# A graph network on one Trainium2 core: the first group's weights, messages and low parts put in another order

## The chip, the core and the metric

The kernel runs on one core of one Trainium2 chip. The metric is the device time of one execution in microseconds (us), the median of several runs. The engines are named as the profile names them: PE (TensorE: matrix products, PEld its weight loads), DVE (VectorE), ACT (ScalarE), POOL (GpSimd), SP (SyncE, which here only issues transfers). Each engine runs its own instructions in the order of the program and waits on semaphores for the others.

## What is computed

The inputs are 32 graphs of 256 nodes with 128 features (`x`) and a 256 by 256 adjacency matrix for each (`adj`), all in 32-bit floating point. The reference, cut to what matters:

```python
x = layernorm(x + gnn0(x, adj));  x = layernorm(x + gnn1(x, adj))

# gnn0
h = relu(bn1(conv1d(xc, conv1_w, pad=0)))          # xc: x with features first
h = bn2(conv1d(h, conv2_w, pad=8))                 # 17 taps along the 256 nodes
x_conv = relu(h + xc)
s = x @ w_se.T + b_se                              # 3 numbers a node
A = exp(-squared_distance(s, s)) * adj
x_nmp = A @ relu(x @ w_msg.T + b_msg)              # messages
gi = concat(x_conv, x_nmp) @ w_ih.T + b_ih;  gh = x @ w_hh.T + b_hh
r, z = sigmoid(gi_r + gh_r), sigmoid(gi_z + gh_z)
out0 = (1 - z) * tanh(gi_n + r * gh_n) + z * x

# gnn1
out1 = relu(((1 + eps) * x + adj @ x) @ W1 + b1) @ W2 + b2
```

## The kernel before

**Groups and steps.** The 32 graphs are handled in 8 groups of 4. The work on a group has a front (first convolution, 17-tap convolution, messages, distances, message sum) and a back (gates, the two norms, the adjacency product, the two-layer net). A prologue does the front of group 0 alone and begins that of group 1; step s then does the back of group s-1 between pieces of the front of group s; a last part does the back of group 7. In each engine's program the order is written out by hand in the functions `prologue`, `steady` and `last`; nothing but semaphores ties the engines together.

**High and low parts.** A large product is done as three products of rounded operands: every 32-bit operand is split into a high part (made by ACT, functions with `high` in their name, tiles `wh`, `xh`, `sth`, `w1h`) and the rest, the low part (a subtraction, so far always on DVE: `wl`, `xl`, `stl`, `w1l`). PE takes high x high, low x high and high x low, in `products` (line 1074).

**The 17 taps.** The convolution is cut into nine smaller ones, `taps(g, n)` for n from 0 to 8, of 4 or 5 taps each, three on each of three streams of data (M, A, B). Their weights are the taps themselves (`c2raw`, in the space of `tail`), sums of two neighbours (`msum`, in the space of `gbuf`) and sums in the tile `qsum` (in the space of `adjT[1]`): slots 0 to 4, 5 to 9 and 10 to 13. The prologue makes these sums, then for each n the high part (`tap_high(n)`, ACT) and the low part (`tap_low(n)`, DVE); PE waits for the n-th low part on the semaphore `w_low`. The streams are the relu of the first convolution (`h1_out` on ACT, tile `h1`) and differences of it that POOL makes: `split_diff` (tile `dx`, two instructions), `diff_a` and `diff_b` (tile `dv`). Their parts are made by `odd_high`, `diff_high`, `odd_low` and `diff_low`.

**What else POOL does.** It multiplies the exponentials with the adjacency matrix (`mask`, four a group) and adds 1 + eps to the diagonal of the adjacency matrix (`add_diagonal`, four a group, 128x256).

**The end of the prologue.** PE does the first convolution of group 1 (`conv1(1, 1, 0)` and `conv1(1, 1, 1)`) and the message sums (`nmp`), between the last taps of group 0. ACT writes the two halves of group 1's `h1` from it (line 578). Before the first taps of group 1 PE waits for the low parts of the gate weights (`graw`, nine slots, 128x1152) and of W1 (128x256), the 11th and 12th count of `w_low`; both are subtractions on DVE.

**Transfers.** SP issues all loads and stores, ACT only the load of the identity matrix. The order on SP is: vectors and first weights, x of group 0 in two halves, the 17 taps (`c2raw`, 1088 KB), later weights, adjacency of group 0, gate weights, x of group 1.

## Time and profile before

| | us |
|---|---|
| median of three runs (lowest, highest) | 415.11 (414.59, 415.78) |
| the profiled execution's own time | 415.75 |
| span of its trace | 413.9 |
| PE busy | 380.0 (92%) |
| DVE busy | 309.7 (75%) |
| POOL busy | 224.3 (54%) |
| ACT busy | 211.1 (51%) |

The span is what the trace covers, from the first instruction to the last; the execution's own time is longer by what lies around it, 1.85 us here. Busy times are of the span. PE shows busy during most of it, but a row of PE lasts until its modelled end while the next has begun, so the spacing of its rows tells more than their length.

### The profile page before, as it was taken

Reading aid. Unit: us, or ns where it says so; the run is one execution under the profiler, and the core shown is the slowest. Engines: PE = TensorE matmul, PEld = TensorE weight load, DVE = VectorE, ACT = ScalarE, POOL = GpSimd, SP = SyncE. Lnnn points to the kernel's source line nnn. Section 1 sums busy time; section 2 is a strip of 40 time slices with the busy share of each in tenths; the row PEclk is TensorE's granted clock in tenths of the full one; section 3 lists DMA queues with packets and bytes.
Section 4 is the critical chain, followed back from the end, with each engine's and each line's share of the span. In section 5 each row is a group of like instructions: output and inputs, shape, how many; then the busy total and the mean of one; then the engine's idle time right before and its main releaser. Section 6 shows DMA issues by size and latency. Waiting matters only on the chain.

```text
span 413.9 us, 6658 instructions
## 1 busy us (share of the span) xinstructions
PE 380.0 (92%) x2369; PEld 338.3 (82%) x2369; DVE 309.7 (75%) x599; ACT 211.1 (51%) x366; POOL 224.3 (54%) x215
## 2 busy tenths in 40 slices
PE   2479999998999999998999999999999999999974
PEld 1478888898898898988898988988988988989864
DVE  3878847879588885888688795878768795867665
ACT  3637456642755337443566427653484436461641
POOL 2536544848357464657349473565556573495252
PEclk9989999999999999999999999999999999999999
DMA  7302001110012000130012010120001300000101
GB/s 270 155 2 102 2 1 51 41 64 25 26 52 103 24 29 0 53 101 25 25 51 73 29 44 7 51 101 25 27 6 46 104 25 28 1 2 0 52 0 51
DMA packets 7561, 19.40 MB, mean 47 GB/s; under 512 B 625, under 2 KB 4977, under 8 KB 6385
## 3 DMA queue, kind: packets, MB, share of 16 engines
q1 hardware_dynamic: 7392, 19.02, 13.2%
q8 instruction: 14, 0.23, 0.2%
q14 instruction: 11, 0.08, 0.1%
q10 hardware_dynamic: 144, 0.07, 0.1%
HBM read 14.89 MB, written 4.19 MB: 46 GB/s over the span
## 4 chain that ended last, share of the span: by engine, by line
PE 57%; DVE 23%; issue 8%; POOL 5%; ACT 4%; DMA 2%; SPq 0%; DVEq 0%; POOLq 0%; ACTq 0%
PE back L1074 28%; PE conv L1074 14%; PE back L1236 6%; DVE tail L882 5%; POOL rstd L472 4%; PE front L1149 3%; DVE xn L882 3%; PE front L1121 2%; DMA tail<-in_conv_dram 2%; DVE esum L839 2%; DVE usum L843 2%; DVE usum L827 2%; DVE wl L925 1%; DVE stats L872 1%; DVE stl L765 1%
## 5 line engine op out<-in xcount | busy, mean ns | idle before, releaser
L1074 PE MATMUL conv<-sth,wh 128*128 128x256 f32 x320 | 99.5, 311 | 16.5 <-DVE stl L765 13.1
L1074 PE MATMUL conv<-stl,wh 128*128 128x256 f32 x320 | 92.8, 290 | 0.0
L1074 PE MATMUL conv<-sth,wl 128*128 128x256 f32 x320 | 92.7, 290 | 0.0
L1074 PEld LDWEIGHTS conv<-sth,wh 128*128 128x128 f32 x320 | 62.2, 194 | 20.6 <-DVE wl L925 10.4
L472 POOL TENSOR_TENSOR rstd<-rstd,minus_half 128x4 f32<-128x4 f32 (+1 forms) x34 | 36.1, 1062 | 65.2 <-DVE rstd L876 65.2
L1074 PEld LDWEIGHTS conv<-stl,wh 128*128 128x128 f32 x320 | 62.3, 195 | 1.0
L1074 PEld LDWEIGHTS conv<-sth,wl 128*128 128x128 f32 x320 | 62.1, 194 | 0.0
L477 POOL TENSOR_TENSOR xw<-xw,xv 128x512 f32<-128x512 f32 (+1 forms) x17 | 20.9, 1228 | 62.0 <-ACT xw L640 62.0
L490 POOL TENSOR_TENSOR amat<-amat,adjT 128x512 f32<-128x512 f32 x32 | 48.1, 1525 | 5.1 <-ACT amat L616 4.2
L882 DVE TENSOR_SCALAR tail<-tail,stats,rstd 128x128 f32<-128x128 f32 x64 | 41.4, 709 | 0.0
L647 ACT ACTIVATE xch<-usum 128x512 fp32r<-128x512 f32 x16 | 10.1, 631 | 40.7 <-DVE usum L843 40.7
L455 POOL TENSOR_TENSOR dx<-dv 128x272 f32<-128x272 f32 x16 | 14.7, 916 | 29.8 <-DVE stl L765 29.8
L1149 PE MATMUL front<-amat,msg 128*128 128x256 f32 x128 | 30.2, 379 | 0.0
L1236 PE MATMUL back<-later_w,tail 128*128 128x128 f32 x240 | 29.2, 275 | 0.0
L1149 PE MATMUL back<-adjT,xn 128*128 128x256 f32 x120 | 29.1, 385 | 0.0
L1236 PEld LDWEIGHTS back<-later_w,tail 128*128 128x128 f32 x240 | 28.6, 192 | 0.6
L578 ACT ACTIVATE h<-conv,bn 128x512 f32<-128x512 f32 x16 | 12.5, 781 | 27.6 <-PE conv L1074 27.1
L1149 PEld LDWEIGHTS front<-amat,msg 128*128 128x128 f32 x128 | 23.7, 189 | 3.2
L622 ACT ACTIVATE msg<-msg 128x384 f32<-128x384 f32 (+1 forms) x24 | 10.9, 484 | 29.8 <-DVE msg L785 29.4
L848 DVE SCALAR_TENSOR_TENSOR xcl<-usum,xch 128x512 fp32r<-128x512 f32 x16 | 22.2, 1388 | 4.9 <-ACT xch L647 4.9
L858 DVE TENSOR_TENSOR gbuf<-back,gbuf 128x512 f32<-128x512 f32 x14 | 9.7, 692 | 20.6 <-PE back L1074 20.6
L765 DVE TENSOR_TENSOR stl<-dx,sth 128x544 fp32r<-128x544 f32 x24 | 17.7, 737 | 9.8 <-ACT sth L565 9.7
(198 smaller groups left out, 987.1 us busy)
## 6 DMA issues: line engine op xcount, KB each, us to landing
adjT<-in_adj_dram SPq DMA_DIRECT2D x8, 1024.0 KB, 4.8
out_dram<-tail SPq DMA_DIRECT2D x15, 256.0 KB, 2.2
xv<-in_x_dram SPq DMA_DIRECT2D x7, 512.0 KB, 3.3
tail<-in_conv_dram SPq DMA_DIRECT2D x1, 1088.0 KB, 8.2
gbuf<-in_gates_dram SPq DMA_DIRECT2D x1, 576.0 KB, 11.8
xv<-in_x_dram SPq DMA_DIRECT2D x2, 256.0 KB, 3.0
later_w<-in_later_dram SPq DMA_DIRECT2D x1, 452.0 KB, 8.9
out_dram<-tail SPq DMA_DIRECT2D x2, 128.0 KB, 1.9
```

Of the source, the lines that this page charges most:

```text
L455: done(pool.tensor_tensor(dx[:, 0, :, :], ev, od, ALU.subtract), DX_READY[st])
L472: done(pool.tensor_tensor(rstd[:, k, h, q], rstd[:, k, h, q], minus_half[:, q], ALU.pow), RSTD[k])
L477: done(pool.tensor_tensor(xw[:, h, part(c)], xw[:, h, part(c)], xv[u][:, part_cols(h, c)], ALU.mult), XWX_READY)
L490: done(pool.tensor_tensor(amat[:, b, :, :], amat[:, b, :, :], adjT[u][:, b, :, :], ALU.mult), A_READY)
L578: done(act.activation(h1[:, 2 * h:2 * h + 2, :, :, PAD:PAD + TQ].rearrange("p b r q m -> p (b r) q m"), conv1_bank(h)[:, :].rearrange("p ( ...
L622: done(act.activation(msg_blocks[:, q0:q1, :], msg_blocks[:, q0:q1, :], ACT.Relu), MSG_READY)
L765: done(dve.tensor_tensor(dst, src, full(hi), ALU.subtract), name)
L848: done(dve.scalar_tensor_tensor(xcl[:, :, par, :], pre[:, :, par, :], 0.0, full(xch[:, :, par, :]), ALU.max, ALU.subtract), XCL_READY)
L882: last = dve.tensor_scalar(dst(q), src(q, q + 1), stats[:, k, h, q, 1:2], rstd[:, k, h, q:q + 1], ALU.subtract, ALU.mult)
L1074: ins = pe.matmul(bank, a, b, start=first and k == 0, stop=last and k == len(todo) - 1)
L1149: ins = pe.matmul(tile[:, k * N:(k + 1) * N], lhs(b, rm), rhs(b, rm), start=rm == 0, stop=rm == PAR - 1)
L1236: ins = pe.matmul(bank("out", h, c)[:, k * P:(k + 1) * P], hid[:, h, f, q * P:(q + 1) * P], w2[:, f, :], start=f == 0, stop=f == 1)
```

## The change

**Transfers.** The 17 taps come in four transfers, two issued by SP and two by ACT ahead of the identity matrix, all counted on `conv2_loaded`. SP waits for all four before it issues the adjacency matrix, x of group 1 and (now after x) the gate weights.

**Messages.** PE does group 0's messages right after the first convolution, ahead of the first taps, and the transposed factors ahead of `taps(0, 3)`. DVE's additions on the messages stand between the first low parts.

**Sums and low parts.** The two sums of 512 elements for `qsum` slots 5 to 8 and 10 to 13 go from DVE to POOL, as do the low parts of the gate weights and of W1. Those two have a semaphore of their own, `w_gate_low`, and PE waits for its second count where it waited for the 12th of `w_low`.

**Order.** On POOL two masks of group 0 stand ahead of the last `split_diff` of group 0. On ACT and DVE several parts move, among them both halves of group 1's x (`x_high`, `x_low`) ahead of the last difference of group 0's stream B, and the constant `diag` to a later place.

The core of the diff:

```diff
@@ SP
-                sp.dma_start(c2raw, t["conv2"]).then_inc(conv2_loaded, 16)
+                sp.dma_start(c2raw[:, 0:5, :], t["conv2"][:, 0:5, :]).then_inc(conv2_loaded, 16)
+                sp.dma_start(c2raw[:, 5:9, :], t["conv2"][:, 5:9, :]).then_inc(conv2_loaded, 16)
                 sp.dma_start(later_w[:, :], t["later"]).then_inc(later_loaded, 16)
+                sp.wait_ge(conv2_loaded, 64)
                 load_adj(0, 0)
-                sp.dma_start(graw, t["gates"]).then_inc(gates_loaded, 16)
                 wait(sp, X_LOADED, 0, 16)
                 load_x(1, 1)
+                sp.dma_start(graw, t["gates"]).then_inc(gates_loaded, 16)
@@ POOL
                 split_diff(0, 0)
+                pool.wait_ge(conv2_loaded, 64)
+                pool.tensor_tensor(qsum[:, 5:9, :], c2raw[:, 0:TAPS - 1:4, :], c2raw[:, 2:TAPS:4, :],
+                                   ALU.add).then_inc(tap_sums_ab, 1)
                 diff_a(0)
+                pool.tensor_tensor(qsum[:, 10:14, :], c2raw[:, 1:TAPS:4, :], c2raw[:, 3:TAPS:4, :],
+                                   ALU.add).then_inc(tap_sums_ab, 1)
                 split_diff(0, 1)
                 diff_b(0)
+                mask(0, 0, 0)
+                mask(0, 0, 1)
                 split_diff(0, 2)
-                for b in range(GB):
-                    mask(0, 0, b)
-                pool.wait_ge(bn_ready, 3)
+                mask(0, 0, 2)
+                mask(0, 0, 3)
+                pool.wait_ge(w_high, 11)
+                pool.tensor_tensor(wl[:, S_GATE:S_GATE + 9, :], graw, full(wh[:, S_GATE:S_GATE + 9, :]),
+                                   ALU.subtract).then_inc(w_gate_low, 1)
                 split_diff(1, 0)
                 diff_a(1)
                 split_diff(1, 1)
                 diff_b(1)
+                pool.wait_ge(bn_ready, 3)
                 for b in range(GB):
                     add_diagonal(0, 0, b)
+                pool.wait_ge(w_high, 12)
+                pool.tensor_tensor(w1l[:, :], w1raw, full(w1h[:, :]), ALU.subtract).then_inc(w_gate_low, 1)
@@ ACT
+                act.dma_start(c2raw[:, 9:13, :], t["conv2"][:, 9:13, :]).then_inc(conv2_loaded, 16)
+                act.dma_start(c2raw[:, 13:TAPS, :], t["conv2"][:, 13:TAPS, :]).then_inc(conv2_loaded, 16)
                 act.dma_start(ident, t["consts"]).then_inc(consts_loaded, 16)
@@ DVE
-                dve.wait_ge(gates_loaded, 16)
-                w_low_part(wl[:, S_GATE:S_GATE + 9, :], graw, wh[:, S_GATE:S_GATE + 9, :], 11)
-                w_low_part(w1l[:, :], w1raw, w1h[:, :], 12)
@@ PE
                 conv1(0, 0, 1)
+                pe.wait_ge(later_loaded, 16)
+                messages(0, 0)
                 pe.wait_ge(w_low, 2)
                 taps(0, 0)
                 pe.wait_ge(w_low, 3)
                 taps(0, 1)
-                pe.wait_ge(later_loaded, 16)
-                messages(0, 0)
                 pe.wait_ge(w_low, 4)
                 taps(0, 2)
+                pe.wait_ge(consts_loaded, 16)
+                factors(0)
                 pe.wait_ge(w_low, 5)
                 taps(0, 3)
-                pe.wait_ge(consts_loaded, 16)
-                factors(0)
...
                 nmp(0, 1)
                 taps(0, 8, 1)
-                pe.wait_ge(w_low, 12)
+                pe.wait_ge(w_gate_low, 2)
```

POOL, from the last differences of group 0 to the first instruction of step 1 (tile `xw`), before. `amat` are the masks of group 0, `dx` and `dv` the differences (ahead of the masks those of group 0, behind them those of group 1), `diag` is 1 + eps on the diagonal; in brackets stand the semaphores that an instruction waits for.

```order
L455 TENSOR_TENSOR dx<-dv 128x272 [waits streamA_ready,h1_diff_ready]
L456 TENSOR_TENSOR dx<-dv 128x272
L490 TENSOR_TENSOR amat<-amat,adjT 128x512 [waits adj_loaded,exp_ready] x4
L455 TENSOR_TENSOR dx<-h 128x272 [waits streamB_ready,h1_ready,bn_ready]
L456 TENSOR_TENSOR dx<-h 128x272
L461 TENSOR_TENSOR dv<-h 128x544 [waits streamA_ready,h1_ready]
L455 TENSOR_TENSOR dx<-dv 128x272 [waits streamM_ready,h1_diff_ready]
L456 TENSOR_TENSOR dx<-dv 128x272
L465 TENSOR_TENSOR dv<-h 128x4x68 [waits streamB_ready]
L466 TENSOR_TENSOR dv<-h 128x4x68
L498 TENSOR_TENSOR adjT<-adjT,diag 128x2x128 [waits a_ready] x4
L477 TENSOR_TENSOR xw<-xw,xv 128x512 [waits x_weight_ready]
```

The same place after the change, from behind the last two masks on, with line numbers of the changed file.

```order
L530 TENSOR_TENSOR wl<-gbuf,wh 128x1152 [waits w_high]
L459 TENSOR_TENSOR dx<-h 128x272 [waits streamB_ready,h1_ready]
L460 TENSOR_TENSOR dx<-h 128x272
L465 TENSOR_TENSOR dv<-h 128x544 [waits streamA_ready,h1_ready]
L459 TENSOR_TENSOR dx<-dv 128x272 [waits streamM_ready,h1_diff_ready]
L460 TENSOR_TENSOR dx<-dv 128x272
L469 TENSOR_TENSOR dv<-h 128x4x68 [waits streamB_ready]
L470 TENSOR_TENSOR dv<-h 128x4x68
L502 TENSOR_TENSOR adjT<-adjT,diag 128x2x128 [waits a_ready,bn_ready]
L502 TENSOR_TENSOR adjT<-adjT,diag 128x2x128 [waits a_ready] x3
L540 TENSOR_TENSOR w1l<-later_w,w1h 128x256 [waits w_high]
L481 TENSOR_TENSOR xw<-xw,xv 128x512 [waits x_weight_ready]
```

What moved: the gate weights' low part (`wl`) stands between the masks and group 1's first differences, and W1's low part (`w1l`) is the last instruction of POOL's prologue, behind group 1's differences and the four diagonal additions. The masks, four in a row in the first list, stand two ahead of and two behind the first list's first two rows.

DVE, from the sums of the taps to the first difference's low part, before. `adjT` holds the tile `qsum` here, `gbuf` the tile `msum`, `tail` the taps.

```order
L954 TENSOR_TENSOR gbuf<-tail 128x1024 [waits conv2_loaded]
L956 COPY gbuf<-tail 128x128
L957 COPY adjT<-tail 128x2x128
L959 TENSOR_TENSOR adjT<-gbuf 128x512 [waits tap_pairs]
L960 TENSOR_TENSOR adjT<-tail 128x512
L961 TENSOR_TENSOR adjT<-tail 128x512
L925 TENSOR_TENSOR wl<-adjT,wh 128x640 [waits w_high]
L765 TENSOR_TENSOR stl<-h,sth 128x272 [waits streamM_high_ready]
L925 TENSOR_TENSOR wl<-gbuf,wh 128x640 [waits w_high]
L925 TENSOR_TENSOR wl<-gbuf,wh 128x512 [waits w_high]
L765 TENSOR_TENSOR stl<-dx,sth 128x544 [waits streamM_high_ready]
```

After, from the third sum on (`msg` and `fact` are the additions on the messages):

```order
L976 TENSOR_TENSOR adjT<-gbuf 128x512 [waits tap_pairs]
L806 TENSOR_TENSOR msg<-front,later_w 128x384 [waits msg_full,factors_set,later_loaded]
L808 TENSOR_TENSOR fact<-front,later_w 128x6x3
L946 TENSOR_TENSOR wl<-adjT,wh 128x640 [waits w_high]
L786 TENSOR_TENSOR stl<-h,sth 128x272 [waits streamM_high_ready]
L806 TENSOR_TENSOR msg<-front,later_w 128x384 [waits msg_full]
L808 TENSOR_TENSOR fact<-front,later_w 128x6x3
L946 TENSOR_TENSOR wl<-gbuf,wh 128x640 [waits w_high]
L806 TENSOR_TENSOR msg<-conv,later_w 128x256 [waits msg_full]
L808 TENSOR_TENSOR fact<-conv,later_w 128x4x3
L946 TENSOR_TENSOR wl<-gbuf,wh 128x512 [waits w_high]
L786 TENSOR_TENSOR stl<-dx,sth 128x544 [waits streamM_high_ready]
```

What moved: two sums have left DVE, and the additions on the messages, which stood behind the last row of the first list, stand between the low parts.

## Rows read from the trace of the kernel before

**Rows 1.** Windows, one step: stretch, length, busy by engine, granted clock, DMA, GB/s.

```profile
143.41:191.52 48.11, 46.74 (x293) 41.59 (x293) 37.44 (x71) 25.16 (x43) 27.50 (x25) 1.00 0.14 45
```

**Rows 2.** PE's timeline: start, length, line, tiles, count, [idle before, releaser].

```profile
15.52 0.55 PE L1074 MATMUL conv<-sth,wh 128*128 128x256 f32 x1 [6.74 <-DVE stl L765]
...
28.11 0.55 PE L1074 MATMUL conv<-sth,wh 128*128 128x256 f32 x1 [2.78 <-DVE wl L925]
...
36.24 0.39 PE L1074 MATMUL conv<-sth,wh 128*128 128x256 f32 x1
...
40.41 0.47 PE L1074 MATMUL conv<-xh,wh 128*128 128x512 f32 x1 [0.97 <-DVE xl L765]
```

**Rows 3.** PE's timeline, first taps of group 1 (first, last) and the next.

```profile
46.78 0.28 PE L1074 MATMUL conv<-sth,wh 128*128 128x256 f32 x1
...
48.48 0.28 PE L1074 MATMUL conv<-sth,wl 128*128 128x256 f32 x1
49.46 0.36 PE L1074 MATMUL conv<-sth,wh 128*128 128x256 f32 x1 [0.69 <-DVE esum L839]
```

**Rows 4.** Windows, columns as in rows 1: PE at its slower pace.

```profile
15.50:21.30 5.80, 5.57 (x25) 5.32 (x26) 3.62 (x3) 3.94 (x8) 4.47 (x5) 1.00 0.01 5
...
28.15:31.55 3.40, 3.40 (x17) 3.40 (x18) 3.40 (x5) 0.00 (x0) 1.93 (x2) 0.55 0.02 5
```

**Rows 5.** ACT's timeline: first exponentials of group 0; second half of group 1's h1.

```profile
34.24 1.09 ACT L616 ACTIVATE amat<-front 128x512 f32<-128x512 f32 x2 [0.42 <-PE front L1141]
...
44.15 0.78 ACT L578 ACTIVATE h<-conv,bn 128x512 f32<-128x512 f32 x1 [0.44 <-PE conv L1074]
```

**Rows 6.** POOL's timeline: masks of group 0, then group 1's differences and the diagonals.

```profile
34.92 6.49 POOL L490 TENSOR_TENSOR amat<-amat,adjT 128x512 f32<-128x512 f32 x4 [4.20 <-ACT amat L616]
...
45.06 0.76 POOL L455 TENSOR_TENSOR dx<-h 128x272 f32<-128x272 f32 x1 [3.65 <-issue]
...
48.79 0.76 POOL L455 TENSOR_TENSOR dx<-dv 128x272 f32<-128x272 f32 x1 [0.73 <-DVE stl L765]
...
52.60 2.79 POOL L498 TENSOR_TENSOR adjT<-adjT,diag 128x256 f32<-128x256 f32 x4
```

**Rows 7.** DVE's timeline in the first group.

```profile
10.40 1.22 DVE L954 TENSOR_TENSOR gbuf<-tail 128x1024 f32<-128x1024 f32 x1 [3.27 <-DMA tail<-in_conv_dram]
...
13.08 0.68 DVE L961 TENSOR_TENSOR adjT<-tail 128x512 f32<-128x512 f32 x1
13.68 0.82 DVE L925 TENSOR_TENSOR wl<-adjT,wh 128x640 fp32r<-128x640 f32 x1
...
22.89 0.56 DVE L785 TENSOR_TENSOR msg<-front,later_w 128x384 f32<-128x384 f32 x1 [3.77 <-PE front L1121]
...
33.85 0.73 DVE L765 TENSOR_TENSOR stl<-dx,sth 128x544 fp32r<-128x544 f32 x1
...
37.01 0.75 DVE L839 SCALAR_TENSOR_TENSOR esum<-conv,bn,ams 128x512 f32<-128x512 f32 x1
37.79 0.78 DVE L843 TENSOR_TENSOR usum<-usum,esum 128x512 f32<-128x512 f32 x1
38.49 3.46 DVE L765 TENSOR_TENSOR xl<-xv,xh 128x512 fp32r<-128x512 f32 x2
41.88 1.34 DVE L925 TENSOR_TENSOR wl<-gbuf,wh 128x1152 fp32r<-128x1152 f32 x1
43.15 0.41 DVE L925 TENSOR_TENSOR w1l<-later_w,w1h 128x256 fp32r<-128x256 f32 x1
```

**Rows 8.** POOL by line and shape: count, busy us, mean ns, idle before.

```profile
L477 POOL TENSOR_TENSOR xw<-xw,xv 128x512 f32<-128x512 f32 x15 | 19.4, 1294 | 58.5 <-ACT xw L640 58.5
```

**Rows 9.** Transfers until 10.37 us: packets and bytes; KB, us to landing.

```profile
DMA packets 926, 2.81 MB, mean 271 GB/s; under 512 B 94, under 2 KB 350, under 8 KB 725
...
tail<-in_conv_dram SPq DMA_DIRECT2D x1, 1088.0 KB, 8.2
```

More of the change, by code:

```diff
@@ L278, in gnn_kernel @@
         w_low = sem("w_low")
+        w_gate_low = sem("w_gate_low")
+        tap_sums_ab = sem("tap_sums_ab")
         def wait(eng, name, g, j):
@@ L949, in prologue @@
                 dve.tensor_copy(gbias[:, 3:4], vec[:, BIH + 2:BIH + 3]).then_inc(bn_ready, 1)
-                dve.scalar_tensor_tensor(diag[:, :], ident, vec[:, EPS1:EPS1 + 1], ident,
-                                         ALU.mult, ALU.add).then_inc(bn_ready, 1)
-                dve.wait_ge(conv2_loaded, 16)
+                dve.wait_ge(conv2_loaded, 64)
                 dve.tensor_tensor(msum[:, 0:NM - 1, :], c2raw[:, 0:TAPS - 1:2, :], c2raw[:, 1:TAPS:2, :],
@@ L959, in prologue @@
                 dve.tensor_tensor(qsum[:, 0:4, :], msum[:, 0:NM - 1:2, :], msum[:, 1:NM:2, :], ALU.add).then_inc(tap_sums, 1)
-                dve.tensor_tensor(qsum[:, 5:9, :], c2raw[:, 0:TAPS - 1:4, :], c2raw[:, 2:TAPS:4, :], ALU.add)
-                dve.tensor_tensor(qsum[:, 10:14, :], c2raw[:, 1:TAPS:4, :], c2raw[:, 3:TAPS:4, :], ALU.add).then_inc(tap_sums, 1)
+                dve.wait_ge(later_loaded, 16)
+                dve.wait_ge(factors_set, 2)
+                messages(0, 0)
                 tap_low(0)
                 odd_low(0, 0)
+                messages(0, 1)
                 tap_low(1)
+                messages(0, 2)
                 tap_low(2)
                 diff_low(0, 0)
-                dve.wait_ge(later_loaded, 16)
-                dve.wait_ge(factors_set, 2)
-                for k in range(3):
-                    messages(0, k)
                 factors(0)
                 tap_low(3)
+                odd_low(0, 1)
                 tap_low(4)
                 tap_low(5)
-                odd_low(0, 1)
+                m_sum(0)
                 diff_low(0, 1)
-                m_sum(0)
                 tap_low(6)
+                odd_low(0, 2)
                 tap_low(7)
                 tap_low(8)
-                odd_low(0, 2)
+                x_low(1, 1, 0)
+                x_low(1, 1, 1)
                 diff_low(0, 2)
@@ L985, in prologue @@
                 pre_sum(0, 0)
-                x_low(1, 1, 0)
-                x_low(1, 1, 1)
-                dve.wait_ge(gates_loaded, 16)
-                w_low_part(wl[:, S_GATE:S_GATE + 9, :], graw, wh[:, S_GATE:S_GATE + 9, :], 11)
-                w_low_part(w1l[:, :], w1raw, w1h[:, :], 12)
+                dve.wait_ge(consts_loaded, 16)
+                dve.scalar_tensor_tensor(diag[:, :], ident, vec[:, EPS1:EPS1 + 1], ident,
+                                         ALU.mult, ALU.add).then_inc(bn_ready, 1)
                 xconv_low(0, 0)
@@ L1244, in prologue @@
                 conv1(0, 0, 1)
+                pe.wait_ge(later_loaded, 16)
+                messages(0, 0)
                 pe.wait_ge(w_low, 2)
```

28 lines of the change are left out of this document (15 added, 13 removed).

## The prediction

> **What bounds the kernel now.** I read the windows of whole steps first. A step takes 48.1 us and PE is busy for 46.7 of them [rows 1]: from step 1 on the kernel goes at PE's pace, and the one idle microsecond of a step comes from a chain inside that step. So the change, all of it in the prologue, can move the end of the program only by moving the moment at which PE begins group 1's taps and runs on. Before, the first of them starts at 46.78, the last of `taps(1, 0)` at 48.48, 0.12 us apart, and `taps(1, 1)` at 49.46, held up by an addition of DVE [rows 3].
>
> Then I read the prologue on PE's timeline. PE waits 6.74 us for the first taps' low parts, 2.78 us for tap set 3's, 0.97 us ahead of group 1's first convolution; tap set 6 begins at 36.24 and that convolution at 40.41 [rows 2]. On DVE's timeline the reader is to see why: it waits for the taps until 10.40 and for PE's messages 3.77 us, and is otherwise packed [rows 7]. The taps land 8.2 us after their issue, when 2.81 MB have moved [rows 9], while first weights, x of group 0 and taps are only 1.71 MB by their shapes.
>
> **The stall that the change adds.** PE's wait at the end of the prologue is now for POOL's second low part. Behind it in PE's queue stand group 1's taps and messages and the gates of group 0; ACT's first convolution result, DVE's message additions and later the stores wait for those. On POOL, W1's low part stands behind group 1's seven difference instructions and the four diagonal additions. Before, that chain starts at 45.06, right after ACT has written the second half of group 1's h1 (44.15 + 0.78 = 44.93) [rows 5, 6]. It is stopped once, until 48.79, by a low part of DVE that no part of the change brings forward, and its last diagonal addition ends at 52.60 + 2.79 = 55.39 [rows 6]. Nobody waited for that end before: W1's low part was made on DVE at 43.15, in 0.41 us [rows 7].
>
> Price of the added instruction: 256 elements like one diagonal addition, 2.79 / 4 = 0.70 us. So, with h1 of group 1 at its old time, PE is released at 56.1 instead of passing at 46.78: **+9.35 us**. Nothing of PE's own lies beside it: the message sums and last taps of group 0 run out at about 46.9.
>
> What this gives back: by 56.1 the inputs of `taps(1, 1)` are long there, so its stall goes: 49.46 - 48.48 - 0.12 = **-0.86**.
>
> What it costs beside: after 2.78 us without work PE's products ran at the lower of its two clock levels, granted 0.55 on average, 17 products in 3.40 us; after the 6.74 us, 25 products took 5.80 us, the same slow pace, although the column prints 1.00 there [rows 2, 4]. At 0.121 us each these would have taken 2.1 and 3.0 us. An idle stretch of 9 us will be followed by such a stretch of tap products, which costs between 1.3 and 2.8 us: I take **+2.0**, in the middle.
>
> **Does the rest bring group 1's h1 forward?** Step by step, in the times of the trace:
>
> The taps' arrival. The adjacency matrix (1 MB) no longer shares the DMA engines with them, since SP waits; two of the four transfers start earlier on ACT's queue, beside x. The 2.81 MB from 2.13 (the issue) to 10.37 are 0.34 MB a us, at which 1.71 MB would be there at 7.2; a gain of nothing leaves 10.37. I take 9.5, nearer to the row, since the slowest of the engines that carry the transfer decides its landing. What waits behind SP's new wait (adjacency, x of group 1, gate weights) lands some 5 to 8 us later than the taps, by about 17, and is first used at about 28; hidden. The two transfers on ACT's queue may delay ACT's first work and x of group 0 by up to 1 us; the wait for the taps hides it.
>
> The Trainium skill (DMA: Bandwidth & Descriptors, Issuing engines are not separate DMA queues) says that transfers issued by several engines run on the same 16 DMA engines. By that alone the split gains nothing, the taps stay at 10.37, and the sum grows by at most 0.9.
>
> First tap set. Two sums of 0.68 leave DVE [rows 7], but POOL takes 1.29 us for a multiplication of 512 elements [rows 8] and does them while DVE makes its own sums. Side by side with POOL's masks two subtractions of 512 elements took 3.46 us, where alone one takes 0.68 [rows 7]: each such meeting costs DVE about a microsecond. With a message addition of 0.56 ahead of the first low part too, the first taps start at about 15.9, as before (15.52). No gain yet.
>
> Messages. PE does them while it waits for the first low parts, so the 3.77 us of DVE's wait, PE's 2.78 us of idle time and the slow stretch after it go. Tap set 3 starts at about 24 instead of 28.11, tap set 6 at about 30.1 instead of 36.24: a lead of 6 us. The first exponentials come at about 28.3 instead of 34.24 [rows 2, 5].
>
> Given back. POOL now does two masks (1.29 each) ahead of stream B's last differences: 28.8 + 2.6 + two differences of 0.76 to 1.2 = 33.5; ACT's high part and DVE's low part (0.73) end at 35, where the latter began at 33.85 before [rows 7]. Tap set 7 starts at 35.1 against 37.7 before: the lead is 2.6 us. Then DVE's two x sums run beside masks 2 and 3, some 1.7 us each like the rows above, and the addition that frees the bank ends at about 39.1; before it ended at 37.76 and the convolution waited for something later, until 40.41 [rows 2, 7]. It starts at about 39.2: a lead of 1.2 us. And PE has idled 3.4 us ahead of tap set 7, longer than the 2.78 that lowered its clock before, so about 1.2 us go to slow products there. **Net 0** for group 1's h1, bounds -4 (meetings milder, clock kept) and +2 (taps at 10.37, slow products throughout).
>
> The rest is covered: the gate weights' low part leaves DVE (1.34 us, rows 7) and costs POOL 1152 / 512 x 1.29 = 2.9 us, but POOL idled 3.65 us ahead of group 1's differences [rows 6, 7]; if that cover were gone, it would add to the stall one for one. `diag` moves to a place in DVE's wait, and its user comes 10 us later.
>
> **The sum.** 9.35 - 0.86 + 2.0 + 0 = +10.5. Against the profiled execution's own 415.75 that is 426.2; this execution lies 0.64 above the median of the three runs (415.11), from which I forecast **425.6 us**, with 423 to 428.5 for this case alone.
>
> **Rivals.**
>
> Lead kept: DVE's and POOL's meetings cost less than I think and 4 to 6 us of the lead survive. Against it speaks the pair of subtractions beside the masks (3.46 us); for it, that not every DVE instruction of the new order meets one of POOL. The stall is then 4 to 6 us shorter: 419.6 to 422. Chance 0.12.
>
> Faster: W1's low part comes in time. POOL's chain from h1 to it is 11.2 us (44.93 to 56.1), so PE passes unhindered only if h1 of group 1 is written 8.5 us earlier, by 36.4. Group 1's convolution would then have to start by 32, about when tap set 6 ends. From there on the kernel would be about 0.9 faster, 414. Tap sets 7, the x sums and the masks all stand ahead of it: chance 0.02. A standstill, with the lead between: 0.02.
>
> Full exclusion: where a DVE instruction with two SBUF inputs meets one of POOL, one of them waits out the whole of the other, so that a pair takes 1.29 + 0.68 = 1.97 us. The trace has 3.46 / 2 = 1.73 [rows 7, 8]. With some 8 meetings in the new order this adds 1.9 us: 427.5, and with a late landing 429.5. Chance 0.07. That is the rule of the Trainium skill (SBUF — State Buffer, Who interferes with whom: an exclusive lock); the trace agrees in direction, but with less.
>
> That the transfers do not come earlier at all changes the forecast by 0.9 and stands in its range.
>
> **How the numbers follow.** The forecast 0.77, lead kept 0.12, exclusion 0.07, the two others 0.04. The range reaches from the lead kept to the forecast's upper end: 420.8 to 428.5, with about 0.17 left out. A change of 0.3% (1.25 us) is about what a measurement tells from none. Slower by more than that: 0.77 + 0.12 + 0.07 = 0.96; same 0.02, faster 0.02.
>
> **What would show it.** In the new profile: PE idle for about 9 us around 47 to 56, released by POOL's W1 subtraction; POOL's chain unbroken from h1 to it, 11 us; products at the lower clock behind it, and no stall at `taps(1, 1)`; tap set 6 near 30, tap set 7 near 35; DVE's message wait gone. The forecast fails if W1's low part ends before 50, if PE's products after the stall are not slowed, or if group 1's h1 is written outside 41 to 47.

## The result, and the profile after

The changed kernel takes 426.74 us (median of 6 runs, 426.15 to 429.19); the kernel before, run beside it, 415.06 (413.39 to 415.78). The ratio is 1.0306, with a 95% interval of 1.0277 to 1.0335: slower by 3%. The forecast was 425.6. The profiled execution took 428.27 us, its span is 426.5.

The list of PE's waits of the changed kernel names the cause in its first row (us in total, times, longest).

```profile
PE conv L1090 <- POOL w1l L540: 9.0, 1, 9.0
```

PE's timeline of the changed kernel, the rows that answer to [rows 2, 3]: first taps, tap sets 1, 6 and 7, the first convolution of group 1, the first taps of group 1, and the second tap set of group 2 one step on.

```profile
14.32 0.36 PE L1090 MATMUL conv<-sth,wh 128*128 128x256 f32 x1 [2.62 <-issue]
...
18.59 0.35 PE L1090 MATMUL conv<-sth,wh 128*128 128x256 f32 x1 [2.21 <-DVE stl L786]
...
30.15 0.39 PE L1090 MATMUL conv<-sth,wh 128*128 128x256 f32 x1
...
35.24 0.36 PE L1090 MATMUL conv<-sth,wh 128*128 128x256 f32 x1 [3.35 <-issue]
...
39.44 0.50 PE L1090 MATMUL conv<-xh,wh 128*128 128x512 f32 x1 [2.48 <-DVE esum L860]
...
56.72 0.58 PE L1090 MATMUL conv<-sth,wh 128*128 128x256 f32 x1 [9.02 <-POOL w1l L540]
...
106.50 0.38 PE L1090 MATMUL conv<-sth,wh 128*128 128x256 f32 x1 [1.09 <-DVE stl L786]
```

The reader is to see a lead that comes and goes. Tap set 6 starts at 30.15, where it started at 36.24 [rows 2]: 6 us early. Group 1's convolution starts at 39.44, where it started at 40.41: 1 us early. Then PE stands 9.02 us. The last row has a counterpart in the kernel before, the same wait in the same step, 10.95 us earlier; from there on the steps are the same.

```profile
95.55 0.38 PE L1074 MATMUL conv<-sth,wh 128*128 128x256 f32 x1 [1.08 <-DVE stl L765]
```

POOL's timeline (answers to [rows 6]) and one row of ACT (to [rows 5]) show what PE waits for.

```profile
28.83 2.54 POOL L494 TENSOR_TENSOR amat<-amat,adjT 128x512 f32<-128x512 f32 x2 [7.29 <-ACT amat L632]
31.32 1.21 POOL L459 TENSOR_TENSOR dx<-dv 128x272 f32<-128x272 f32 x1
...
37.92 3.10 POOL L530 TENSOR_TENSOR wl<-gbuf,wh 128x1152 fp32r<-128x1152 f32 x1
45.76 0.76 POOL L459 TENSOR_TENSOR dx<-h 128x272 f32<-128x272 f32 x1 [4.75 <-ACT h L594]
...
49.47 0.76 POOL L459 TENSOR_TENSOR dx<-dv 128x272 f32<-128x272 f32 x1 [0.73 <-DVE stl L786]
...
53.23 2.76 POOL L502 TENSOR_TENSOR adjT<-adjT,diag 128x256 f32<-128x256 f32 x4
55.95 0.72 POOL L540 TENSOR_TENSOR w1l<-later_w,w1h 128x256 fp32r<-128x256 f32 x1
```

```profile
44.90 0.78 ACT L594 ACTIVATE h<-conv,bn 128x512 f32<-128x512 f32 x1 [0.63 <-PE conv L1090]
```

From the end of h1 (45.68) to the end of W1's low part (56.67) POOL's chain takes 10.99 us. It is stopped once, for 0.73 us at 49.47, as it was before [rows 6].

DVE's timeline (answers to [rows 7]) shows no wait for the taps or for PE's messages any more, and two slow pairs, `xl` and `usum`.

```profile
8.42 1.23 DVE L971 TENSOR_TENSOR gbuf<-tail 128x1024 f32<-128x1024 f32 x1
...
30.15 2.92 DVE L786 TENSOR_TENSOR xl<-xv,xh 128x512 fp32r<-128x512 f32 x2 [2.46 <-ACT xh L581]
34.41 0.72 DVE L786 TENSOR_TENSOR stl<-dx,sth 128x544 fp32r<-128x544 f32 x1 [1.34 <-ACT sth L581]
35.06 3.45 DVE L848 TENSOR_TENSOR usum<-xv,esum 128x512 f32<-128x512 f32 x2
38.64 0.75 DVE L860 SCALAR_TENSOR_TENSOR esum<-conv,bn,ams 128x512 f32<-128x512 f32 x1
```

Windows of the changed kernel (columns as in [rows 1]): the first half of group 1's convolution and message sums, the stall, the products behind it, the next such stretch, and the start of the last part.

```profile
40.20:43.70 3.50, 3.50 (x11) 2.80 (x11) 2.31 (x3) 1.33 (x3) 0.81 (x1) 0.54 0.00 0
47.70:56.72 9.02, 0.01 (x1) 0.00 (x1) 4.01 (x5) 1.06 (x2) 8.24 (x10) 0.67 0.00 0
56.72:61.55 4.83, 4.83 (x24) 4.83 (x25) 0.00 (x0) 0.56 (x1) 0.00 (x0) 0.56 0.01 3
61.55:66.40 4.85, 4.85 (x40) 4.72 (x39) 1.70 (x7) 1.02 (x3) 0.00 (x0) 1.00 0.00 0
409.70:413.10 3.40, 3.40 (x11) 2.75 (x10) 1.76 (x5) 0.60 (x1) 3.30 (x5) 0.59 0.00 0
```

Behind the stall the granted clock is at the lower of its two levels for most of 4.83 us (0.56 on average): 24 products there, 40 in the stretch of the same length that follows. The last row belongs to the end of the program: PE idles 2.5 us there in both kernels, and here the clock falls behind it. The product that ends this idle time, before and after:

```profile
397.54 0.41 PE L1200 MATMUL front<-ident_w,gbuf 128*128 128x128 f32 x2 [2.52 <-DVE gbuf L866]
```

```profile
408.54 0.41 PE L1216 MATMUL front<-ident_w,gbuf 128*128 128x128 f32 x2 [2.53 <-DVE gbuf L887]
```

From it to the end of the span it takes 426.5 - 408.54 = 17.96 us, before 413.9 - 397.54 = 16.36. So 1.6 of the 12.6 us between the two spans come from the end, and 10.95 from the prologue. The traces don't put the 1.6 us down to the change. From 95.55 or 106.50, or the same row of each run below, to the end of the span it takes 318.4 us in the kernel before and in E3, which is the changed kernel with PE kept busy, and 319.8 to 320.1 in the changed kernel and the other eleven, E4 among them, which is the kernel before with one part of the change. All have the idle 2.5 us; in the first two the clock doesn't fall behind it.

### The profile page after: what moved, and what is told of

The parts are those of the page before. It is cut to its first block, busy times and chain, and to the rows that moved or that the text cites. A ratio compares the mean times of both kernels' runs of the same rounds, so it can differ in the third digit from the quotient of the medians.

```text
span 426.5 us, 6661 instructions
## 1 busy us (share of the span) xinstructions
PE 383.2 (90%) x2369; PEld 340.6 (80%) x2369; DVE 310.9 (73%) x595; ACT 211.0 (49%) x366; POOL 230.4 (54%) x219
## 4 chain that ended last, share of the span: by engine, by line
PE 56%; DVE 20%; issue 10%; POOL 8%; ACT 4%; DMA 2%; DVEq 0%; SPq 0%; POOLq 0%; ACTq 0%
PE back L1090 27%; PE conv L1090 14%; PE back L1252 6%; DVE tail L903 5%; POOL rstd L476 4%; PE front L1165 4%; DVE xn L903 3%; PE front L1137 2%; DVE stl L786 1%; DVE usum L864 1%; DVE esum L860 1%; DVE stats L893 1%; DVE gbuf L879 1%; DVE hl L786 1%; DMA adjT<-in_adj_dram 1%
## 5 line engine op out<-in xcount | busy, mean ns | idle before, releaser
L494 POOL TENSOR_TENSOR amat<-amat,adjT 128x512 f32<-128x512 f32 x32 | 47.2, 1496 | 9.4 <-ACT amat L632 7.3
L1165 PE MATMUL front<-amat,msg 128*128 128x256 f32 x128 | 31.7, 393 | 0.0
L1165 PEld LDWEIGHTS back<-adjT,xn 128*128 128x128 f32 x120 | 22.1, 193 | 3.5
```

The lines of the kernel that those rows point to most:

```text
L494: done(pool.tensor_tensor(amat[:, b, :, :], amat[:, b, :, :], adjT[u][:, b, :, :], ALU.mult), A_READY)
L1165: ins = pe.matmul(tile[:, k * N:(k + 1) * N], lhs(b, rm), rhs(b, rm), start=rm == 0, stop=rm == PAR - 1)
```

## The experiments

The theory: nearly all of the loss is the place of one instruction, W1's low part, in POOL's queue, and the place of the wait for it in PE's; behind it the clock; and upstream a lead of 6 us is made and given back. The rivals: POOL is overloaded as a whole; the reordering itself costs; the products behind the stall are slow for another reason.

The start of PE's second tap set of group 2 (95.55 before, 106.50 after) is used as a **mark**: from there on every kernel runs at the pace of the steps. It belongs to the one execution that was traced, whose own time stands beside it: where that time is far from the median (E2, E7, E10), the mark says little of the kernel. Below, "early" is the kernel with W1's low part made early (E1), the base of most of the others.

| | edit | median us | ratio to before, 95% interval | mark, us | traced, us |
|---|---|---|---|---|---|
| before | | 415.06 | | 95.55 | 415.75 |
| after | the change | 426.74 | 1.0306 (1.0277, 1.0335) | 106.50 | 428.27 |
| E1 | W1's low part early on POOL | 416.85 | 1.0069 (1.0039, 1.0098) | 94.52 | 416.25 |
| E2 | PE waits for it only in step 1 | 418.41 | 1.0074 (1.0045, 1.0103) | 97.50 | 419.21 |
| E3 | PE kept busy in the stall | 426.23 | 1.0271 (1.0210, 1.0332) | 105.54 | 425.93 |
| E4 | before, W1's low part last on POOL | 424.31 | 1.0251 (1.0191, 1.0312) | 102.69 | 424.40 |
| E5 | early, last differences ahead of masks | 416.11 | 1.0023 (0.9989, 1.0056) | 94.00 | 415.71 |
| E8 | E5, x's high parts ahead of exponentials | 415.65 | 1.0031 (1.0002, 1.0059) | 94.00 | 415.68 |
| E6 | early, one transfer of the taps | 419.21 | 1.0103 (1.0067, 1.0140) | 97.27 | 419.02 |
| E9 | early, no wait of SP | 418.20 | 1.0074 (1.0049, 1.0099) | 97.28 | 419.06 |
| E7 | early, sums on DVE | 417.49 | 1.0042 (1.0018, 1.0066) | 93.39 | 415.11 |
| E10 | E8, masks behind DVE's addition | 414.27 | 0.9978 (0.9960, 0.9996) | 95.76 | 417.54 |
| E11 | path cleared | 412.43 | 0.9947 (0.9916, 0.9978) | 90.39 | 412.01 |
| E12 | E11, masks not put off | 412.62 | 0.9934 (0.9908, 0.9961) | 90.94 | 412.83 |

**E1 and E2: the place of the instruction, and that of the wait.**

```diff
@@ POOL (E1)
                                    ALU.subtract).then_inc(w_gate_low, 1)
+                pool.wait_ge(w_high, 12)
+                pool.tensor_tensor(w1l[:, :], w1raw, full(w1h[:, :]), ALU.subtract).then_inc(w_gate_low, 1)
                 split_diff(1, 0)
...
                     add_diagonal(0, 0, b)
-                pool.wait_ge(w_high, 12)
-                pool.tensor_tensor(w1l[:, :], w1raw, full(w1h[:, :]), ALU.subtract).then_inc(w_gate_low, 1)
@@ PE (E2)
-                pe.wait_ge(w_gate_low, 2)
+                pe.wait_ge(w_gate_low, 1)
...
+                if isinstance(s, int) and s == 1:
+                    pe.wait_ge(w_gate_low, 2)
                 mlp1(gb, 0)
```

> The changed kernel, but POOL makes W1's low part directly behind the gate weights' low part, ahead of group 1's differences. My theory (the place of this one instruction costs nearly all): it ends at about 41.8 us, so PE passes the end of the prologue as soon as its own work runs out (47.7 us in the trace of the changed kernel, 46.9 before). The idle 9.02 us and the slow products behind it go, the small stall at the second tap set of group 1 comes back (up to 0.9): about 416, between 415 and 417, that is 0 to 0.5% above the kernel before. Rival (POOL as a whole is overloaded): group 1's first taps then wait for POOL's differences instead, and the time stays above 419.

> The changed kernel with every instruction of POOL, DVE and ACT in its place; PE waits at the end of the prologue for the gate weights' low part only, and for W1's low part in step 1, ahead of the first product that reads it. My theory (the wait stands too early in PE's queue): the same as with W1's low part made early, 415 to 417, with the subtraction still ending near 56.7 us in the trace. Rival (POOL's late chain holds PE by something else as well, the differences or the diagonals): over 419, with a new wait of PE on POOL between 47 and 57 us.

In both the stall is gone. E1 on PE's timeline: the last of the first taps of group 1, and the second tap set.

```profile
47.44 0.28 PE L1090 MATMUL conv<-sth,wl 128*128 128x256 f32 x1
48.41 0.36 PE L1090 MATMUL conv<-sth,wh 128*128 128x256 f32 x1 [0.69 <-DVE esum L860]
```

The small stall at the second tap set is back (0.69, as in [rows 3]), and it starts 1.05 us earlier than before. In E2 the subtraction stays late on POOL, and nobody waits for it:

```profile
57.27 0.74 POOL L540 TENSOR_TENSOR w1l<-later_w,w1h 128x256 fp32r<-128x256 f32 x1
```

```profile
51.37 0.36 PE L1090 MATMUL conv<-sth,wh 128*128 128x256 f32 x1 [0.65 <-DVE esum L860]
```

E1's 416.85 lies in its expected range and E2's 418.41 above it, below the rival's 419; their intervals overlap. The theory holds: POOL as a whole is not late, only this instruction is, and only because PE asks for it ahead of work that doesn't need it. But both ratios, 1.0069 and 1.0074, lie clear above 1, where 0 to 0.5% was expected of E1: what is left of the change costs some 3 us.

E2's mark is 3 us behind E1's, and PE waits for POOL in neither. The order upstream is the same; 0.80 us of the difference are there when tap set 7 starts (35.92 and 35.12). Then the clock is at its lower level from about 34.4 to 44.7 in the profiled execution of E2, and in that of E1 from 34.6 to 38.0 alone. The windows of E2, and of E1 behind its slow stretch:

```profile
34.80:45.05 10.25, 7.82 (x25) 6.61 (x26) 7.94 (x7) 4.28 (x9) 6.07 (x3) 0.52 0.02 6
```

```profile
38.40:45.00 6.60, 5.67 (x29) 5.00 (x30) 5.54 (x6) 3.07 (x6) 4.62 (x4) 1.00 0.00 1
```

So marks a few us apart may differ by the clock alone, and are compared below together with the rows ahead of them.

**E3: the clock behind the stall.**

```diff
+                for k in range(36):
+                    pe.matmul(bb[0][:, :], wh[:, 0, :], xh[0][:, cols(k % 2)], start=True, stop=True)
                 pe.wait_ge(w_gate_low, 2)
```

> The changed kernel with 36 extra products of 512 columns on PE ahead of the wait, into a bank that the gates write anew: about 8.3 us of extra work inside the 9.02 us of idle time. My theory: PE is released at the same 56.7 us, but the products behind it run at 0.12 us each from the start; the cost of the clock goes and nothing else, so about 2.2 us less than the changed kernel, 424 to 425. Rival (the products after the stall are slow for another reason, such as loads or transfers beside them): no change, within 0.5 us of the changed kernel. If the products themselves delay something, more than 427.

PE is released at 57.57, and the clock stays up behind it (windows of E3):

```profile
57.57:61.55 3.98, 3.98 (x32) 3.98 (x33) 0.00 (x0) 0.57 (x1) 0.00 (x0) 1.00 0.00 0
```

From the release to the mark it takes 105.54 - 57.57 = 47.97 us, in the changed kernel 106.50 - 56.72 = 49.78: the clock costs 1.81 us, near the 2.2 of the theory. The rival, slow for another reason, falls by these rows: the same products, 32 in 3.98 us, with the clock up. The times alone don't show it. The median, 426.23, is above the expected 424 to 425 and 0.5 below the changed kernel's, with intervals overlapping; in the profiled execution the release comes 0.85 us later than in the changed kernel's.

**E4: one part alone, in the kernel before.** The diff moves W1's low part from DVE to the end of POOL's prologue, and PE waits for it.

```diff
-                w_low_part(w1l[:, :], w1raw, w1h[:, :], 12)
@@ POOL, behind add_diagonal
+                pool.wait_ge(w_high, 12)
+                pool.tensor_tensor(w1l[:, :], w1raw, full(w1h[:, :]), ALU.subtract).then_inc(w_gate_low, 1)
```

> The kernel before, with one part of the change alone: W1's low part is the last instruction of POOL's prologue instead of DVE's, and PE waits for it at the end of the prologue. My theory: POOL's chain ends at 55.4 us there, the subtraction at 56.1, so PE stands 9.3 us, runs on at the lower clock (2.0) and saves the 0.86 at the second tap set: 10 to 11 above the kernel before, 425 to 426.5, as much as the whole change. Rival (the reordering upstream pays for part of it, or costs something): below 423 or above 428, the difference to the changed kernel being what the rest is worth.

```profile
52.72 0.72 POOL L527 TENSOR_TENSOR w1l<-later_w,w1h 128x256 fp32r<-128x256 f32 x1
```

```profile
53.54 0.55 PE L1076 MATMUL conv<-sth,wh 128*128 128x256 f32 x1 [9.13 <-issue]
```

PE stands 9.13 us and goes on 0.10 us behind the end of POOL's subtraction. The kernel is 424.31 - 414.5 = 9.8 above the kernel before that ran beside it (10.4 by the ratio), where 10 to 11 was expected. From E4's ratio to that of the whole change, 1.0251 to 1.0306, the intervals overlap, so this pair doesn't say what the rest is worth; E1 and E2 do: some 0.7%.

**E5 and E8: the lead that is given back.**

```diff
@@ POOL (E5, E8)
+                split_diff(0, 2)
                 mask(0, 0, 0)
                 mask(0, 0, 1)
-                split_diff(0, 2)
@@ ACT (E5: diff_high ahead of the exponentials; E8: x_high too)
                 odd_high(0, 2)
+                x_high(1, 1)
+                diff_high(0, 2)
                 exps(0, 0)
...
@@ DVE (E5, E8)
                 tap_low(8)
+                diff_low(0, 2)
                 x_low(1, 1, 0)
                 x_low(1, 1, 1)
-                diff_low(0, 2)
```

> The kernel with W1's low part made early, and the last differences of group 0 again ahead of all four masks on POOL, with their high part (ACT) directly behind the high part of stream B and their low part (DVE) ahead of group 1's x. My theory (the lead at tap set 6 is given back because two masks stand ahead of these differences): POOL makes them at about 25.5 us, when it is idle, tap set 7 follows tap set 6 without the idle 3.35 us, at about 31.7; then x's low parts and the two x sums of DVE, some of them beside masks, hold the bank, and the convolution of group 1 starts at about 36.5 instead of 39.3. About 2.8 us less than with W1 early alone: 413.5 to 415, close to the kernel before. Rival (the lead is lost to slower DVE instructions in any order): the convolution still starts after 38.5 and the time stays within 0.3% of W1 early alone.

> As the kernel before it in this call, and ACT makes the high parts of group 1's x ahead of the exponentials, in 24.8 to 28 us, when it is idle. My theory: DVE then has x's low parts and both x sums behind it before most of the masks run, the bank is free by about 32 to 33, the convolution of group 1 starts at 33 to 34 (39.3 with W1 early alone) and group 1's first taps at 42 to 43: 5 to 6 us less than W1 early alone, 410.5 to 412.5, below the kernel before by 0.6 to 1.1%. Rival (from there on POOL's masks and the gate weights' low part hold PE, since they do not move): group 1's first taps wait for POOL and start after 45; then 413 to 415.

In E5 tap set 7 follows tap set 6 without a wait, as expected, and the convolution starts at 37.17 rather than 39.33 in E1. But its time (416.11) is above the expected 413.5 to 415, and E8 brings the convolution no further (37.21, not 33 to 34): both parts of E8's expectation fail. Its rival fails too: 415.65 is above the 415 that it allowed, and PE doesn't wait for POOL. In E5 the clock takes another part: it is at its lower level when the convolution and the message sums run (window below), so the second tap set starts at 47.88, only 0.53 ahead of E1.

```profile
37.90:41.30 3.40, 3.40 (x11) 2.68 (x9) 2.76 (x3) 1.30 (x2) 1.96 (x2) 0.56 0.01 2
```

DVE's timeline of E8, and POOL's:

```profile
29.44 3.47 DVE L786 TENSOR_TENSOR xl<-xv,xh 128x512 fp32r<-128x512 f32 x2
32.83 3.44 DVE L848 TENSOR_TENSOR usum<-xv,esum 128x512 f32<-128x512 f32 x2
```

```profile
29.20 6.52 POOL L494 TENSOR_TENSOR amat<-amat,adjT 128x512 f32<-128x512 f32 x4 [1.47 <-ACT amat L632]
```

All four DVE instructions meet the four masks, 1.73 us each, where one takes 0.68 alone [rows 7]. So the changed kernel gives its lead back in two places: 3.35 us of PE's idle time to the masks ahead of the differences, and then to the two x sums beside masks (3.45 us), behind which PE waits 2.48 us for `esum`. Where E5 and E8 take the first away, the second grows: PE then idles 3.48 us for `esum`.

**E10: the meetings taken away.** POOL begins the masks only behind DVE's addition `esum`.

```diff
                 split_diff(0, 2)
+                wait(pool, G_READY, 0, 1)
                 mask(0, 0, 0)
```

> The kernel with the x parts early, and POOL begins the four masks of group 0 only when DVE has made the addition that frees the bank for group 1's convolution. The same instructions, none of them beside the others' any more. My theory (what ate the lead is that each 512-element instruction of DVE takes 1.7 instead of 0.7 us beside a mask): x's low parts take 1.4 us together instead of 3.47, the x sums 1.4 instead of 3.44; the addition ends near 33 instead of 37.1, the convolution of group 1 starts at 33.5 to 34.5 instead of 37.2. The message sums then wait some 1.3 us for the masks, and group 1's first taps start at 43 to 44.5 instead of 47.2 (as the trace counts them, the last of the first set at 46.9 before this edit): 3 to 4 us less than without the wait, 411.5 to 413. Rival (the masks are on the path themselves, so that putting them off costs what the meetings cost): group 1's first taps start within 1 us of before the edit and the time is the same within 0.3%.

```profile
31.08 1.29 DVE L787 TENSOR_TENSOR xl<-xv,xh 128x512 fp32r<-128x512 f32 x2
32.29 1.29 DVE L849 TENSOR_TENSOR usum<-xv,esum 128x512 f32<-128x512 f32 x2
```

```profile
43.07 0.94 POOL L534 TENSOR_TENSOR w1l<-later_w,w1h 128x256 fp32r<-128x256 f32 x1
43.97 0.77 POOL L459 TENSOR_TENSOR dx<-h 128x272 f32<-128x272 f32 x1
```

```profile
48.16 0.36 PE L1091 MATMUL conv<-sth,wh 128*128 128x256 f32 x1 [2.00 <-DVE esum L861]
```

The pairs take 1.29 us instead of 3.47 and 3.44: the meetings are shown. The convolution starts at 34.90 instead of 37.21, the first taps of group 1 at 44.06, as the theory had it, though that is only 1.2 us earlier than in E8 (45.26; the expectation took it to be 47.2). Yet the second tap set starts at 48.16, no earlier than in E8 (47.90): the two low parts of weights now stand in POOL's queue when h1 is there (41.58), and group 1's differences wait for them until 43.97. The theory's cause holds; part of its gain is lost, by another queue than the rival had. The median, 414.27, is above the expected 411.5 to 413, but by the ratios E10 is 0.5% below E8, some 2 us, with intervals that don't meet. The mark, 1.76 us later than E8's, doesn't speak against it: the traced execution, 417.54, is the slowest of E10's 13. It began its first taps 0.63 later, and its clock is at the lower level from 15.5 to 18.9 and again, behind the 2.00 us of idle time, from 49.7 to 53.1.

**E6, E9 and E7: the transfers and the sums.** E6 loads the taps in one transfer, with SP's wait; E9 in four, without it; E7 makes the two sums on DVE.

> The kernel with W1's low part made early, but the 17 taps come in one transfer of SP again; SP still waits for them before it issues the adjacency matrix. My theory (half of the earlier landing is the split, half the wait): they land at 9 to 9.5 us instead of 8.5, and the first taps start up to 1 us later; time plus 0.3 to 1. Rival, by the Trainium skill (DMA: Bandwidth & Descriptors, Issuing engines are not separate DMA queues: all issuers share the same engines): the wait alone does it, and the taps land within 0.3 us of the four transfers.

> The kernel with W1's low part made early, with the four transfers of the taps, but SP does not wait for them before it issues the adjacency matrix, group 1's x and the gate weights. My theory: the adjacency matrix shares the engines with them again, they land at 9.5 to 10.4 us (8.5 with the wait, 10.4 before), and the first taps start 1 to 1.9 us later; the time grows by 0.5 to 1.5. Rival (the split does it): they land within 0.3 us of 8.5 and nothing else moves.

> The kernel with W1's low part made early and the two sums of 512 elements back on DVE, ahead of the first low part, where they stood before the change. My theory (a sum on POOL costs DVE about what it takes off it): DVE's first low parts are shorter again (0.8 and 0.9 instead of 1.2 and 1.5 us) and the sums cost it 1.3; the first taps start within 0.4 us of 14.5, the time is the same within 0.3%. Rival (DVE is relieved): first taps at 15.7 or later, the time 1.2 us longer.

The last transfer of the taps to land (KB, us from issue to landing) and DVE's first sum of them, E6:

```profile
tail<-in_conv_dram SPq DMA_DIRECT2D x1, 1088.0 KB, 7.2
```

```profile
9.37 1.23 DVE L968 TENSOR_TENSOR gbuf<-tail 128x1024 f32<-128x1024 f32 x1 [1.26 <-DMA tail<-in_conv_dram]
```

E9, and the transfer of the changed kernel:

```profile
tail<-in_conv_dram SPq DMA_DIRECT2D x1, 256.0 KB, 6.2
```

```profile
8.80 1.23 DVE L970 TENSOR_TENSOR gbuf<-tail 128x1024 f32<-128x1024 f32 x1
```

```profile
tail<-in_conv_dram SPq DMA_DIRECT2D x1, 256.0 KB, 5.8
```

One transfer is issued at 2.13 us, the last of the four at 2.61, so what counts is the moment of landing: 10.4 before [rows 7, 9], 9.4 in E6, 8.8 in E9 and 8.4 in the changed kernel. The wait alone gives 1.0, the four transfers alone 1.6, both 2.0. So my theory for E6's landing (9 to 9.5) holds and its rival falls, that for E9 (9.5 to 10.4) falls: the four transfers do more than the wait. They differ from the one in three things, their number, ACT as a second issuer and an earlier issue of two of them (0.74 and 1.19 us), and no run takes these apart. The rule that I cited in E6 (the Trainium skill: DMA: Bandwidth & Descriptors, Issuing engines are not separate DMA queues), that transfers of all issuers share the same engines, is therefore not tested here; what falls is only what I drew from it, that the wait alone does it. The first taps start at 15.08 in E6 and 14.80 in E9 (14.52 in E1). What that is worth at the end can't be told: E9's ratio is E1's, E6's interval overlaps it.

In E7 the first taps start at 14.02 (14.52 in E1), slightly earlier than the expected 0.4 us around 14.5, tap set 1 at 17.62 (18.79), and the ratio is 1.0042: within the expected 0.3% of E1; the rival's 1.2 us more falls. The mark is 1.13 earlier, in the fastest of E7's 12 executions. POOL's sums relieve DVE of twice 0.68 us [rows 7] and slow three subtractions beside them by more: 1.20, 1.50 and 1.35 us in E1, 0.82, 0.99 and 0.68 in E7.

**E11 and E12: what the runs point to.** E11 is E10 with the sums on DVE, x's parts ahead of the last differences' parts, and this order on POOL:

```diff
@@ POOL
                 mask(0, 0, 3)
-                pool.wait_ge(w_high, 11)
-                pool.tensor_tensor(wl[:, S_GATE:S_GATE + 9, :], graw, full(wh[:, S_GATE:S_GATE + 9, :]),
-                                   ALU.subtract).then_inc(w_gate_low, 1)
...
                 split_diff(1, 0)
                 diff_a(1)
+                pool.wait_ge(w_high, 11)
+                pool.tensor_tensor(wl[:, S_GATE:S_GATE + 9, :], graw, full(wh[:, S_GATE:S_GATE + 9, :]),
+                                   ALU.subtract).then_inc(w_gate_low, 1)
                 split_diff(1, 1)
                 diff_b(1)
+                pool.wait_ge(w_high, 12)
+                pool.tensor_tensor(w1l[:, :], w1raw, full(w1h[:, :]), ALU.subtract).then_inc(w_gate_low, 1)
@@ PE, step 1
+                    pe.wait_ge(w_gate_low, 1)
                 gates(gb, ub, 0)
...
+                    pe.wait_ge(w_gate_low, 2)
                 mlp1(gb, 0)
```

> What the runs so far point to, put together: the sums on DVE; x's parts ahead of the last differences' parts; the masks behind DVE's bank-freeing addition; on POOL the first differences of group 1 ahead of the gate weights' low part, and W1's low part ahead of the diagonals; PE waits for these two low parts only where it reads them, in step 1. My theory (DVE beside POOL and the order of POOL's queue set the start of group 1): x's low parts and x sums take about 1.4 us each pair, the addition ends near 32.5, group 1's convolution follows tap set 7 at about 34.5 without a wait, its h1 is there by 39.5, and the second tap set of group 1 starts at 44 to 45.5 (48.4 with W1 early alone, 49.5 in the kernel before): 410 to 412, below the kernel before by 0.8 to 1.3%. Rival (a wait that has not shown yet, or the lower clock behind PE's idle stretches, takes it back): within 0.3% of the kernel with the masks put off, about 414.

> The same as the other kernel of this call, but POOL begins the masks as soon as the exponentials are there, so that they run beside DVE's x parts and x sums. My theory: the x sums take 3.4 us together again instead of 1.4, the bank-freeing addition ends 1.5 to 2.5 us later, the convolution of group 1 waits for it by about 1.5 us: 1 to 2 us longer than the other. Rival (masks earlier, message sums earlier, so the meetings pay for themselves): the same within 0.3%, or faster.

```profile
44.25 0.36 PE L1088 MATMUL conv<-sth,wh 128*128 128x256 f32 x1 [0.52 <-DVE esum L855]
```

The second tap set of group 1 starts at 44.25, where the theory had 44 to 45.5 and the kernel before 49.46; the mark is 5.2 us earlier than before. The ratios, 0.9947 and 0.9934, put both below the kernel before (and 3.5% below the changed one); 412.43 is 0.4 above the expected range, and 0.5% below the kernel before is less than the 0.8 to 1.3% expected. Which of E11's parts give how much is not shown; E12 takes away only the masks' wait. E12 shows E11's theory on DVE (x sums 3.47 us instead of 1.29) and not in the time: its rival, the same, is right. The message sums no longer wait for the masks (0.79 us in E11); that this pays for the slower sums is my reading, for E12's traced execution started its first taps 1.57 us later than E11's, so that their later rows don't compare.

## Why the prediction was right

**The stall** (+9.35; by its own rows the term is 55.39 + 0.70 - 46.78 = 9.31). PE is released at 56.72, forecast 56.1, by POOL's W1 subtraction at the end of a chain of 10.99 us (11.2 forecast) that is stopped once, where it was stopped before. That is 9.94 later than before: 9.02 us of idle time, and PE's own work ends 0.92 later. The mechanism is as forecast. E4 shows that this one place costs 9.8 us (10.4 by its ratio), E1 and E2 that some 3 us of the loss are left without it.

**The wait at `taps(1, 1)`** (-0.86): gone behind the stall, back in E1 where the stall is gone.

**The clock** (+2.0): 1.81 by E3, within the bounds of 1.3 to 2.8.

**Group 1's h1** (net 0, bounds -4 and +2): written at 45.68 instead of 44.93, +0.75. The slow products came in another place than forecast: those of tap set 7 ran with the clock up, and it fell behind PE's wait for `esum` (0.54 on average from 40.20 to 43.70), so that from the convolution's start to h1's second half it took 5.46 us instead of 3.74. Most steps on the way came as told: tap set 6 at 30.15 (30.1), tap set 7 at 35.24 (35.1), the addition's end at 39.39 (39.1), the convolution at 39.44 (39.2), the gate weights' low part 3.10 us (2.9) in POOL's idle time, of which 4.75 us were left. Off were the first: the taps landed before 8.42, not at 9.5, and the first taps started at 14.32, not 15.9. PE then stood 2.21 us ahead of tap set 1, for DVE, which I had not foreseen; so the start was better than forecast and the lead at tap set 6 the same.

**The sum**: 56.72 - 46.78 = 9.94 for the later start; from there to the mark 49.78 us instead of 48.77, which is 1.81 for the clock less 0.80 for the missing wait (E3: 47.97). Together the mark moved by 10.95; the forecast sum was 10.5. The medians are 11.68 apart, and the ratio makes it 12.7. The sum has no term for the end of the program, 1.6 us in the profiled executions, which the traces tie to whether the clock fell there and not to the change. How often it does so in the kernel before isn't known, since one execution of it was traced.

**What was put at nothing.** That the rest of the change moves the end by nothing is not borne out by E1 and E2: without the stall both are 0.7% (0.4 to 1.0) above the kernel before. By the ratio the forecast is 2.2 us short; its range had room for that. The cause of the 3 us is not shown. In the traces of the new order PE idles 3.35 us ahead of tap set 7, and the clock falls there or behind the next wait, for 3.4 us in E1, 3.4 in the changed kernel and 10.2 in E2. E1's twelve times lie in two clusters, 416.25 to 416.95 and 418.26 to 419.18, about as far apart as these lengths would put them, and the traced execution is of the first; that the clock parts them is likely, but only one execution was traced.

**The rivals.** Lead kept: refuted by group 1's h1, and E5 to E10 show where it goes. Faster: only with more of the order changed, in E11 and E12. Full exclusion: a pair beside the masks took 3.45 us, 1.73 each as in [rows 7], not 1.97. Its time, 427.5, is nearer to the measured 426.74 than the forecast's 425.6, so the time doesn't decide; its price per meeting is not borne out.

## What to carry to other kernels

An instruction moved to a less busy engine stands behind everything in that engine's queue; what counts is not the engine's share of busy time but what the queue waits for ahead of it, here a chain of 11 us that began with another group's data. Put a wait for a weight at the first product that reads it, not at the end of a stage. And a lead won early in a chain is worth what is left of it at the last wait that all work passes: follow it row by row before counting it.

## What the runs showed of the hardware

DVE and POOL beside each other did not always take turns. With the masks they did, 1.73 us for each DVE instruction. But a POOL subtraction of 272 elements that takes 0.76 us alone took 3.85 in E11. It began beside a DVE subtraction that had begun at 24.29, five more followed that one without a gap, and it ended 0.63 us after the last of them, `xl`, had ended at 27.73. POOL's row, and the first and the last of DVE's:

```profile
24.51 3.85 POOL L459 TENSOR_TENSOR dx<-dv 128x272 f32<-128x272 f32 x1 [3.81 <-DVE stl L781]
```

```profile
24.29 0.68 DVE L941 TENSOR_TENSOR wl<-adjT,wh 128x512 fp32r<-128x512 f32 x1
...
26.45 1.28 DVE L781 TENSOR_TENSOR xl<-xv,xh 128x512 fp32r<-128x512 f32 x2
```

E12 has the same (3.85 us, until 0.64 after DVE's end), E10 2.63. By the rule of the Trainium skill (SBUF — State Buffer, Who interferes with whom: whoever comes first holds the shared ports for the whole instruction) I would expect POOL to get its turn after one; here it ended only when DVE had paused. The cause of the difference between the two cases stays open.

In these traces the clock fell in or behind idle times of PE of 2.0 to 9.1 us, in some executions and not in others: behind 2.78 us in the kernel before, and not behind 2.77 at the same place in E4. The length differs too: in E1 and E2, with the same order up to there, it was at the lower level for 3.4 and for 10.2 us. E1 and E2 have marks 3 us apart, and the intervals of the ratios above reach 0.2 to 0.6% to either side.
